# Whole numbers as weights for the last 128 inputs of batch 1's gate and up products

## The chip, the cores and the metric

The kernel runs on one core of a Trainium2 chip. The metric is the device time of one execution in microseconds. One core has TensorE (PE), VectorE (DVE), ScalarE (ACT), GpSimd (POOL) and SyncE (SP, which here only issues DMAs), each with its own queue of instructions in program order; they meet through semaphores.

## What is computed

Two layers on 2 batches of 512 tokens with 512 features. Each layer is an attention-like block and a feed-forward block, each between layer norms with a residual add. Layer 0's first block is a state space recurrence over the 512 tokens (1024 channels, 16 states); its second is a feed-forward network with 4-bit weights. Layer 1 has an attention over the heads of one token and a mixture-of-experts network. The part that the change is about, cut from the reference:

```python
w[k, n] = q[k, n] * s[g, n] - (z[g, n] + 1) * s[g, n]      # g = k // 128
gate = x2 @ Wg            # [tokens, 512] @ [512, 1376]
up = x2 @ Wu
inter = gate * sigmoid(gate) * up
out = (inter @ Wd).astype(float16)
```

The scale `s` depends on the group g of 128 inputs and on the output n. For one group, x @ W is therefore (x @ (q - z - 1)) times s, with whole numbers as weights.

## The kernel before

**Stages.** Up to about 480 us the recurrence runs: for 16 chunks (8 of each batch, 128 channels each) there are 8 pairs of scans on VectorE (`scan`), fed by ScalarE (`decay`, Exp) and GpSimd (`times_b`), and multiplied by C on VectorE or GpSimd (`times_c`). TensorE sums the states into the PSUM bank `Y_BANK` in four state groups a chunk, and the table `SIDE` says which other matmuls run in which chunk and group: ("out", 0, t) is tile t of batch 0's output projection (16 matmuls). `pair_of(item)` gives the pair at which an item stands, and ScalarE and GpSimd place their own steps by it (copy of the tile, sums, norms). `take_y` on VectorE reads the finished y of a chunk at the second pair of the next.

Then comes the quantized feed-forward, batch 0 (487 to 576 us) and batch 1 (576 to 670 us), then the last layer's network for both batches, with batch 1's attention within it.

**The feed-forward blocks.** The 1376 inner features are 11 blocks (`IC`) of 128. Weights are used as a sum of two float16 halves, and so are the inputs, so each product of 128 inputs takes three matmuls (`halves`: high by high, low by high, high by low) of 512 columns. A block i is: `g` (gate) of 4 x 3 matmuls into a bank of a ring of three, `u` (up) of 12, and the down-projection of block i-1 of 12, in this order on TensorE. A bank of the ring is free for the third next item once its reader has raised `taken`. ScalarE applies SiLU to `g` (`ffn_silu`, into `sg`), VectorE multiplies by `u` from PSUM (`ffn_times`, into `it`, L1440), ScalarE rounds it to float16 (`ffn_high`, `it_hi`, L2188), VectorE subtracts (`ffn_low`, `it_lo`, L1450), and the down-projection of the block waits for that.

**Weights.** Only in batch 0's blocks the weights are made: SP loads a stage (packed words `qw`, zero points and scales `cw`, 1.5 MB as broadcast) into one of four slots (`stage_again`, once the slot is free), VectorE unpacks nibbles (`unpack`, L1262), ScalarE converts (`whole`), VectorE subtracts the zero point (`scaled`, first half: now the slot's `cw[..., 0]` holds q - z - 1 as float16) and multiplies by the scale, ScalarE makes the high half, VectorE the low half. Batch 1 uses the same `gu_hi`, `gu_lo`, `d_hi`, `d_lo`. The scales of the first two blocks are split in two parts at the start of the kernel (`two_parts`, L1374 to L1377).

**Work between the blocks.** In batch 1's blocks VectorE and ScalarE also carry batch 0 on to the last layer: `between(0, i)` on VectorE is the feed-forward's norm and add (i 0 to 2), norms for the transposes (3, 4), attention scores (5), values (6), the attention's add (7) and statistics (8); ScalarE has the matching roots and the softmax's Exp, each with its activation table (`preload_act_table_set`). The order is written out by hand in both queues. TensorE transposes those tiles behind blocks 4 and 9 (`TURN_BEHIND`) and makes qkv in block 5. In batch 0's blocks ScalarE norms batch 1's tiles (`norm_ffn_last`, L1952), and TensorE transposes them one a block from block 7 (`TURN_FIRST`).

## Time and profile before

| | us |
|---|---|
| median of 3 runs | 805.58 |
| lowest and highest | 805.26, 806.01 |
| the profiled execution | 807.46 |
| its span on the core | 805.6 |

| engine | busy us | share of the span |
|---|---|---|
| TensorE, matmuls | 683.4 | 85% |
| VectorE | 688.1 | 85% |
| ScalarE | 469.8 | 58% |
| GpSimd | 480.6 | 60% |

The page gives one execution. Times in it are microseconds from the start of its span. A matmul of 512 columns is listed with a longer duration than the distance to the next one, because they are pipelined; the distance of the starts is what one costs. "[0.91 <-DVE it_lo L1450]" behind a row says that the engine was idle for 0.91 us before it and that the wait ended with that instruction of VectorE. Names are the tiles of the program, without buffer numbers; "x8" is the number of instructions merged into a row. PEclk is the granted clock of TensorE as a share of its full speed.

### The profile page before, as it was taken

How to read it: one execution, taken by the hardware profiler on the slowest of the kernel's cores; microseconds unless marked ns; L12 is line 12 of the kernel's file. 1: busy time of each engine (PE TensorE's matmuls, PEld its weight loads, DVE VectorE, ACT ScalarE, POOL GpSimd, SP SyncE). 2: the span in 40 equal slices, each digit the busy share in tenths (PEclk: the TensorE clock that was granted, in tenths of full speed). 3: DMA queues.
4: the chain of work that ended last, by engine and by line, in shares of the span. 5: the costliest groups of instructions: out<-in, count | busy, mean ns of one | idle time of the engine just before them, and what ended most of it. 6: DMA issues, size and time to landing. Idle time of an engine off the chain costs nothing. (4 is left out here: it accounts for less than half of the span.)

```text
span 805.6 us, 8451 instructions
## 1 busy us (share of the span) xinstructions
PE 683.4 (85%) x2794; PEld 325.1 (40%) x2794; DVE 688.1 (85%) x701; ACT 469.8 (58%) x805; POOL 480.6 (60%) x252
## 2 busy tenths in 40 slices
PE   7979899988687788564637889999999999999995
PEld 6623333323122222111112224444445556887885
DVE  6889999999999999999999998998274576485778
ACT  5478778895656774867664447756325347323333
POOL 2429999999999999999999960220002014331130
PEclk9999979999888997858867989999999999999998
DMA  8434232335503714731235309971040030000011
GB/s 262 92 101 142 75 129 71 119 130 180 186 4 120 246 37 158 229 131 36 96 131 179 102 12 259 256 221 55 1 157 1 1 105 0 1 1 1 0 53 52
DMA packets 42326, 83.19 MB, mean 103 GB/s; under 512 B 6809, under 2 KB 10308, under 8 KB 42028
## 3 DMA queue, kind: packets, MB, share of 16 engines
q1 hardware_dynamic: 42284, 82.66, 32.4%
q8 instruction: 22, 0.36, 0.2%
q14 instruction: 20, 0.16, 0.1%
HBM read 71.43 MB, written 11.21 MB: 103 GB/s over the span
## 5 line engine op out<-in xcount | busy, mean ns | idle before, releaser
L2388 POOL TENSOR_TENSOR dbu<-rep_du,bc 128x1024 f32<-128x1024 f32 x127 | 296.5, 2359 | 1.8 <-ACT rep_du L2054 0.9
L1880 ACT ACTIVATE psum<-rep_dt,aneg 128x512 f32<-128x512 f32 x256 | 166.2, 682 | 117.4 <-DVE hc L1230 96.1
L1219 DVE TENSOR_TENSOR_SCAN psum<-psum,dbu 128x1024 f32<-128x1024 f32 x89 | 203.4, 2285 | 3.4 <-ACT psum L1880 1.5
L970 PE MATMUL psum<-hc,stk 128*32 128x512 f32 x512 | 84.4, 736 | 62.1 <-POOL hc L2397 44.3
L1230 DVE TENSOR_TENSOR hc<-psum,bc 128x1024 f32<-128x1024 f32 x89 | 109.0, 1224 | 3.1
L2397 POOL TENSOR_TENSOR hc<-hc,bc 128x1024 f32<-128x1024 f32 x39 | 91.8, 2355 | 7.7 <-DVE hc L1219 7.7
L1219 DVE TENSOR_TENSOR_SCAN hc<-psum,dbu 128x1024 f32<-128x1024 f32 x39 | 89.0, 2281 | 1.0 <-ACT psum L1880 0.9
L709 PE MATMUL psum<-xf_hi,gu_hi 128*128 128x512 f16 x176 | 66.8, 379 | 0.4 <-ACT sg L2181 0.4
L709 PE MATMUL psum<-xf_hi,gu_lo 128*128 128x512 f16 x176 | 66.8, 379 | 0.0
L709 PE MATMUL psum<-xf_lo,gu_hi 128*128 128x512 f16 x176 | 66.8, 379 | 0.0
L709 PE MATMUL psum<-xT,w_g 128*128 128x512 f32 x120 | 58.7, 636 | 2.6 <-ACT rep_du L2025 2.6
L2465 POOL TENSOR_TENSOR h<-h 128x512 f32<-128x512 f32 x16 | 19.0, 1185 | 70.1 <-ACT h L2296 70.1
L970 PEld LDWEIGHTS psum<-hc,stk 128*32 128x32 f32 x512 | 13.0, 120 | 117.6 <-issue 61.3
L959 PE MATMUL psum<-u,diag 128*32 128x512 f32 x128 | 22.5, 781 | 29.5 <-DVE u L1246 19.9
L2188 ACT CAST it_hi<-it 128x512 f16<-128x512 f32 x22 | 13.6, 617 | 47.0 <-DVE it L1440 47.0
L709 PEld LDWEIGHTS psum<-xT,w_g 128*128 128x128 f32 x120 | 23.3, 204 | 39.5 <-issue 35.4
L1440 DVE TENSOR_TENSOR it<-sg,psum 128x512 f32<-128x512 f32 x22 | 15.0, 683 | 28.2 <-PE psum L709 11.3
L2449 POOL TENSOR_TENSOR w_up_lo<-w_up,w_up_hi 128x1024 fp32r<-128x1024 f32 x4 | 9.4, 2379 | 46.2 <-ACT w_up_hi L2173 46.2
L997 PE MATMUL psum<-d_hi,it_hi 128*128 128x512 f16 x88 | 33.4, 379 | 1.4 <-DVE it_lo L1450 1.4
L2436 POOL TENSOR_TENSOR x<-x,obuf 128x512 f32<-128x512 f32 x4 | 9.3, 2347 | 41.2 <-ACT obuf L1947 41.2
L709 PE MATMUL psum<-xT,w_x 128*128 128x512 f32 x64 | 32.3, 651 | 1.8 <-ACT xT L1764 1.4
L2443 POOL TENSOR_TENSOR w_gate_lo<-w_gate,w_gate_hi 128x32 fp32r<-128x32 f32 x1 | 0.3, 251 | 55.5 <-ACT w_gate_hi L2262 55.5
(305 smaller groups left out, 1453.0 us busy)
## 6 DMA issues: line engine op xcount, KB each, us to landing
rep_dt<-rep_scratch SPq DMA_DIRECT2D x60, 256.0 KB, 3.3
rep_du<-rep_scratch SPq DMA_DIRECT2D x60, 256.0 KB, 4.1
cw<-c_scratch SPq DMA_DIRECT2D x11, 768.0 KB, 12.0
qw<-qgu_in SPq DMA_DIRECT2D x11, 512.0 KB, 6.8
bc<-bc_scratch SPq DMA_DIRECT2D x16, 256.0 KB, 5.0
rep_scratch<-du_t SPq DMA_DIRECT2D x14, 256.0 KB, 2.0
rep_scratch<-dt_t SPq DMA_DIRECT2D x14, 256.0 KB, 2.3
qw<-qd_in SPq DMA_DIRECT2D x11, 256.0 KB, 8.1
```

What stands on the lines that cost most here:

```text
L709: last = pe.matmul(bank(item)[0:rows, cols], lhsT, rhs, start=(n == 0), stop=(n == len(parts) - 1))
L959: last = pe.matmul(y_rows(k), diag[:, k * P // KH:(k + 1) * P // KH], u[b][:, c, :], start=True, stop=False)
L970: last = pe.matmul(y_rows(k), stk[:], hc[:, (i + k // 2) % HCS, k % 2, :], start=False, stop=(s == GN - 1))
L997: last = pe.matmul(psum[:, t, :], v, w, start=(i == 0 and n == 0), stop=(i == IC - 1 and n == 2))
L1219: dve.tensor_tensor_scan(h, a, dbu[:, i % DBS].rearrange("p e t -> p (e t)"), 0.0, ALU.mult, ALU.add)\
L1230: dve.tensor_tensor(hc[:, i % HCS], psum[:, two, :], bc[:, GN + n, :].unsqueeze(1).broadcast_to([P, 2, L]), ALU.mult)\
L1440: dve.tensor_tensor(it[:, k % 2, :], sg[:, k % 2, :], bank(("u", b, i)), ALU.mult)\
L1880: last = act.activation(psum[:, 2 * (i % 2) + e, :], rep_dt[:, cc % 2, k, :], ACT.Exp, scale=aneg[:, k, c, n:n + 1])
L2188: act.copy(it_hi[:, k % 2, :], it[:, k % 2, :]).then_inc(ithi_done, 1)
L2388: pool.tensor_tensor(dbu[:, i % DBS], rep_du[:, cc % 2, k:k + 2, :], bc[:, n, :].unsqueeze(1).broadcast_to([P, 2, L]), ALU.mult).then_inc( ...
L2397: pool.tensor_tensor(hc[:, i % HCS], hc[:, i % HCS], bc[:, GN + n, :].unsqueeze(1).broadcast_to([P, 2, L]), ALU.mult)\
L2465: pool.tensor_tensor(h2[:, k % 2, :], h1[:, k % 2, :], h1[:, k % 2, :], ALU.mult)\
```

## The change

Five edits.

1. The scale splits at the start work on one tile (`s_two`, 12 rows of 256), loaded by two more DMAs, instead of on two tiles. Four VectorE instructions stand where eight stood, and 10 stores where 8 stood.
2. Output tile 3 of batch 0 is computed in state group 2 of chunk 9 instead of group 3. What follows it on ScalarE and GpSimd keeps its place (`OUT_LAST`).
3. `norm_ffn_last` of tiles 0 and 1 moves from block 6 to block 7.
4. For blocks 1 to 10 the whole numbers of the last 128 inputs are copied out of the slot before it is loaded anew (`keep_ints`, 64 KB each), and their scales are loaded transposed, one per output feature (`group16`).
5. In batch 1, blocks 1 to 10, `g` and `u` have 9 matmuls each over the first 384 inputs. The last 128 go through `group_part`: two matmuls with the whole numbers (exact in float16) into `Y_BANK`; ScalarE multiplies the result by the scale of the feature (`group_scaled`) into `sg` or `it`; VectorE adds the bank (`gate_sum`, `up_sum`); SiLU now works on `sg`, and `times_sum` multiplies `sg` by `it`. The places of `gate_sum` and `group_scaled` in the hand-written orders differ by block, two steps of `between` move, and the sum over wq stands ahead of block 0.

```diff
-        (9, 1): [("out", 0, 2)], (9, 3): [("out", 0, 3)],
+        (9, 1): [("out", 0, 2)], (9, 2): [("out", 0, 3)],
...
+OUT_LAST = pair_of(("out", 0, NT - 1)) + 2
...
+        s_two = at("s_two", 205, [AHEAD * P], F16)
+        sa = at("sa", 88.25, [AHEAD * P], F16)
+        sb = at("sb", 88.75, [AHEAD * P], F16)
...
+        ints = {i: at(f"ints{i}", 35 + (i - 1) / 2 if i < 9 else {9: 21.25, 10: 24}[i], [2 * P], F16)
+                for i in range(1, IC)}
+        group16 = at("group16", 206.625, [2, IC], F16)
+        group32 = at("group32", 206.75, [2, IC])
...
                     sp_.wait_ge(split_done, 2)
+                    half = KH // AHEAD
                     sp_.dma_start(c_dram[0:AHEAD, 1, 0:gu].rearrange("i (r n) -> r i n", n=P),
-                                  sa_gu[0:2 * KH, :].rearrange("r (i n) -> r i n", n=P)).then_inc(z_stored, 16)
-                    sp_.dma_start(c_dram[0:AHEAD, 1, gu:], sa_d[0:AHEAD, :]).then_inc(z_stored, 16)
+                                  sa[0:2 * KH, :].rearrange("r (i n) -> r i n", n=P)).then_inc(z_stored, 16)
                     sp_.dma_start(cs_dram[:, 0:gu].rearrange("i (r n) -> r i n", n=P),
-                                  sb_gu[0:2 * KH, :].rearrange("r (i n) -> r i n", n=P)).then_inc(z_stored, 16)
-                    sp_.dma_start(cs_dram[:, gu:], sb_d[0:AHEAD, :]).then_inc(z_stored, 16)
+                                  sb[0:2 * KH, :].rearrange("r (i n) -> r i n", n=P)).then_inc(z_stored, 16)
+                    for i in range(AHEAD):
+                        rows = slice(2 * KH + half * i, 2 * KH + half * (i + 1))
+                        sp_.dma_start(c_dram[i, 1, gu:].rearrange("(r n) -> r n", n=AHEAD * P), sa[rows, :])\
+                            .then_inc(z_stored, 16)
+                        sp_.dma_start(cs_dram[i, gu:].rearrange("(r n) -> r n", n=AHEAD * P), sb[rows, :])\
+                            .then_inc(z_stored, 16)
...
+            def keep_ints(i):
+
+                sp_.wait_ge(q16_used, i + 1)
+                sp_.dma_start(ints[i][:], cw[i % SLOTS][:, 0, 2 * (KH - 1) * P:2 * KH * P]).then_inc(ints_kept, 16)
+
             def stage_again(i):
 
+                if i > SLOTS:
+                    sp_.wait_ge(ints_kept, 16 * (i - SLOTS))
                 sp_.wait_ge(wlo_gu, i - SLOTS + 1)
                 sp_.wait_ge(wlo_d, i - SLOTS + 1)
                 stage(i)
 
             wait_work(sp_, ("out", 1, NT - 1))
             stage(3)
+            keep_ints(1)
             for i in range(SLOTS, IC):
                 stage_again(i)
+                if i > SLOTS:
+                    keep_ints(i - SLOTS + 1)
+            sp_.wait_ge(ints_kept, 16 * (IC - SLOTS))
+            keep_ints(IC - 3)
...
+            keep_ints(IC - 2)
+            keep_ints(IC - 1)
+            for j in range(2):
+                sp_.dma_start(group16[:, j, :], sgu_in[2 * (KH - 1) + j:2 * KH - 1 + j, :]
+                              .rearrange("r (i n) -> n (r i)", n=P),
+                              allow_slow_non_contiguous=True).then_inc(ld_group, 16)
...
+                def group_part(i, j):
+
+                    if i > 1 or j:
+                        pe.wait_ge(group_done, 2 * (i - 1) + j)
+                    else:
+                        pe.wait_ge(ints_kept, 16 * (IC - 1))
+                    w = ints[i][:, j * P:(j + 1) * P]
+                    pe.matmul(psum[:, Y_BANK, :], w, xf_hi[1][:, KH - 1, :], start=True, stop=False)
+                    pe.matmul(psum[:, Y_BANK, :], w, xf_lo[1][:, KH - 1, :], start=False, stop=True)\
+                        .then_inc(group_ready, 1)
...
-                        for kk in range(KH):
+                        for kk in range(KH - 1 if grouped else KH):
                             w = slice((2 * kk + j) * P, (2 * kk + j + 1) * P)
                             parts += halves(gu_hi[:, i, w], gu_lo[:, i, w], xf_hi[b][:, kk, :],
                                             xf_lo[b][:, kk, :])
+                        if grouped:
+                            group_part(i, j)
                         product(item, parts).then_inc(work_ready, 1)
...
+            def two_parts(rows):
+
+                t, d, s = sp_t[0:rows, :], sp_d[0:rows, :], s_two[0:rows, :]
+                link(dve.tensor_scalar(t, s, SPLIT, None, ALU.mult))
+                link(dve.tensor_tensor(d, t, s, ALU.subtract))
+                dve.tensor_tensor(sa[0:rows, :], t, d, ALU.subtract).then_inc(split_done, 1)
+                dve.wait_ge(split_done, 1)
+                dve.tensor_tensor(sb[0:rows, :], s, sa[0:rows, :], ALU.subtract).then_inc(split_done, 1)
...
+            def gate_sum(i):
+                k = IC + i
+                item = ("g", 1, i)
+                wait_work(dve, item)
+                dve.wait_ge(group_done, 2 * i - 1)
+                dve.tensor_tensor(sg[:, k % 2, :], bank(item), sg[:, k % 2, :], ALU.add).then_inc(taken_sem(item), 1)
+
+            def up_sum(i):
+                k = IC + i
+                item = ("u", 1, i)
+                wait_work(dve, item)
+                dve.wait_ge(group_done, 2 * i)
+                dve.tensor_tensor(it[:, k % 2, :], bank(item), it[:, k % 2, :], ALU.add).then_inc(taken_sem(item), 1)
+
+            def times_sum(i):
+                k = IC + i
+                dve.wait_ge(silu_done, i)
+                wait_taken(dve, ("u", 1, i))
+                dve.tensor_tensor(it[:, k % 2, :], sg[:, k % 2, :], it[:, k % 2, :], ALU.mult).then_inc(it_done, 1)
...
+                if b == 0:
+                    gate_sum(6)
...
+                if b == 0:
+                    gate_sum(7)
...
                 if i == 1:
-                    ffn_inv16(b)
-                    ffn_add16(b, 0)
-                    ffn_add16(b, 1)
+                    if b == 0:
+                        ffn_add16(b, 1)
+                        ffn_add16(b, 2)
+                    else:
+                        ffn_inv16(b)
+                        ffn_add16(b, 0)
+                        ffn_add16(b, 1)
                 if i == 2:
-                    ffn_add16(b, 2)
+                    if b:
+                        ffn_add16(b, 2)
                     ffn_add16(b, 3)
...
+            dve.wait_ge(ld_att, 16 * 7)
+            dve.tensor_reduce(wqkv[:, :, 0:DH], wqraw[:], AX.X, ALU.add).then_inc(wq_done, 1)
+            dve.tensor_reduce(bqkv[:, 0:DH], bqraw[:], AX.X, ALU.add).then_inc(wq_done, 1)
+            dve.wait_ge(ld_group, 32)
+            dve.tensor_copy(group32[:], group16[:]).then_inc(group_set, 1)
             for i in range(IC):
+                if i and i not in (6, 7, 8):
+                    gate_sum(i)
                 if i == IC - 1:
                     low_moe(0, [2, 3])
-                ffn_times(1, i)
+                if i:
+                    up_sum(i)
+                    if i == 1:
+                        ffn_inv16(0)
+                        ffn_add16(0, 0)
+                    times_sum(i)
+                else:
+                    ffn_times(1, i)
                 if i == 9:
                     norm_tile("moe", 0, 2, xnc)
                     norm_tile("moe", 0, 3, xnc)
                 ffn_low(1, i)
-                if i == 0:
-                    dve.wait_ge(ld_att, 16 * 7)
-                    dve.tensor_reduce(wqkv[:, :, 0:DH], wqraw[:], AX.X, ALU.add).then_inc(wq_done, 1)
-                    dve.tensor_reduce(bqkv[:, 0:DH], bqraw[:], AX.X, ALU.add).then_inc(wq_done, 1)
                 if i < 8:
                     between(0, i)
                 if i == 7:
+                    gate_sum(8)
                     between(0, 8)
...
+            def group_scaled(i, j):
+
+                k = IC + i
+                if i == 1:
+                    act.wait_ge(group_set, 1)
+                act.wait_ge(group_ready, 2 * (i - 1) + j + 1)
+                if j:
+                    act.wait_ge(itlo_done, k - 1)
+                act.activation((it if j else sg)[:, k % 2, :], psum[:, Y_BANK, :], ACT.Identity,
+                               scale=group32[:, j, i:i + 1]).then_inc(group_done, 1)
+
+            def ffn_silu_sum(i):
+
+                k = IC + i
+                wait_taken(act, ("g", 1, i))
+                act.activation(sg[:, k % 2, :], sg[:, k % 2, :], ACT.Silu).then_inc(silu_done, 1)
...
+                if b == 1 and i >= 1:
+                    if i - 1 not in (0, 2, 5, 6, 8):
+                        group_scaled(i, 0)
+                        group_scaled(i, 1)
+                    ffn_silu_sum(i)
+                else:
+                    ffn_silu(k)
                 if k == 0:
...
-                if k in (TURN_FIRST - 1, TURN_FIRST + 1):
-                    first = k - TURN_FIRST + 1
+                if k in (TURN_FIRST, TURN_FIRST + 1):
+                    first = 2 * (k - TURN_FIRST)
...
+                    if i in (2, 5, 6, 8):
+                        act.preload_act_table_set(LOG_EXP)
+                    if i == 8:
+                        root(("moe", 0), NT)
+                    if i in (0, 2, 5, 6, 8):
+                        group_scaled(i + 1, 0)
+                        group_scaled(i + 1, 1)
                     if i == 0:
                         root16(0)
-                    if i in (2, 5, 6, 8):
-                        act.preload_act_table_set(LOG_EXP)
                     if i == 2:
                         root(("att", 0), NT)
                     if i == 5:
                         att_exp(0)
                     if i == 6:
                         root(("atto", 0), NT)
-                    if i == 8:
-                        root(("moe", 0), NT)
```

## Rows read from the trace of the kernel before

**Rows 1.** busy time by stages: engine, busy us (instructions), granted clock, DMA share, GB/s
```profile
50.00:540.00 490.00, 386.53 (x1392) 132.35 (x1391) 474.77 (x332) 334.34 (x561) 420.46 (x205) 0.87 0.43 136
577.00:669.00 92.00, 91.60 (x457) 45.09 (x455) 52.68 (x100) 39.99 (x60) 9.99 (x7) 1.00 0.16 58
```

**Rows 2.** chain of work that ended last: start us, us, what
```profile
669.56 5.51 PE psum L709 x24
```

**Rows 3.** timeline of TensorE, start of batch 1's block 0: start us, us, engine, line
```profile
576.21 0.38 PE L709 MATMUL psum<-xf_hi,gu_hi 128*128 128x512 f16 x1
576.43 0.38 PE L709 MATMUL psum<-xf_hi,gu_lo 128*128 128x512 f16 x1
```

**Rows 4.** timeline of VectorE, start-up
```profile
44.29 0.28 DVE L1374 TENSOR_SCALAR sp_t<-zs 8x256 f32<-8x256 f16 x1
...
48.62 0.68 DVE L1253 TENSOR_TENSOR ssmn<-ssm,psum 64x512 f32<-64x512 f32 x1
```

**Rows 5.** timelines of ScalarE and VectorE, up to the first scan
```profile
47.27 0.59 ACT L1838 ACTIVATE psum<-rr 64x512 f32<-64x512 f32 x1
...
57.34 2.30 DVE L1219 TENSOR_TENSOR_SCAN psum<-psum,dbu 128x1024 f32<-128x1024 f32 x1 [0.54 <-ACT psum L1880]
```

**Rows 6.** timelines of TensorE, VectorE and GpSimd around output tile 3
```profile
316.24 1.94 PE L970 MATMUL psum<-hc,stk 128*32 128x512 f32 x8 [3.83 <-POOL hc L2397]
318.11 8.80 PE L709 MATMUL psum<-wout,g 128*128 128x512 f32 x16
...
327.98 0.69 DVE L1246 TENSOR_TENSOR u<-u,psum 128x512 f32<-128x512 f32 x1 [1.50 <-PE psum L970]
...
330.94 2.35 POOL L2397 TENSOR_TENSOR hc<-hc,bc 128x1024 f32<-128x1024 f32 x1 [1.88 <-DVE hc L1219]
```

**Rows 7.** busy time by stretches, columns as rows 1
```profile
301.00:304.00 3.00, 3.00 (x16) 0.43 (x8) 3.00 (x2) 1.96 (x4) 3.00 (x2) 0.50 0.76 261
...
315.00:321.00 6.00, 4.76 (x12) 1.58 (x13) 5.96 (x4) 2.60 (x4) 6.00 (x4) 0.50 0.00 0
```

**Rows 8.** timelines of TensorE and ScalarE, batch 0's block 7
```profile
545.98 0.38 PE L997 MATMUL psum<-d_hi,it_hi 128*128 128x512 f16 x1 [0.91 <-DVE it_lo L1450]
...
547.80 0.59 ACT L2181 ACTIVATE sg<-psum 128x512 f32<-128x512 f32 x1
```

**Rows 9.** stage 1 on SP's queue, landing of its last load, unpacking in batch 0
```profile
446.36 0.57 SPq L504 DMA_DIRECT2D qw<-qgu_in  x1
...
cw<-c_scratch SPq DMA_DIRECT2D x1, 768.0 KB, 6.5
...
518.07 1.44 DVE L1262 TENSOR_SCALAR qw<-qw,shift 128x1536 int32<-128x1536 int32 x1
...
551.19 1.01 DVE L1262 TENSOR_SCALAR qw<-qw,shift 128x1536 int32<-128x1536 int32 x1
```

**Rows 10.** costliest groups of the page, an activation scaled per partition
```profile
L1880 ACT ACTIVATE psum<-rep_dt,aneg 128x512 f32<-128x512 f32 x256 | 166.2, 682 | 117.4 <-DVE hc L1230 96.1
```

**Rows 11.** timeline of VectorE, batch 1's blocks 7 and 8
```profile
646.30 2.50 DVE L1512 TENSOR_TENSOR x<-x,on 128x512 f32<-128x512 f32 x4
648.84 2.47 DVE L1159 BATCH_NORM_STATS2 bst<-x 128x6 f32<-128x512 f32 x4
...
651.76 0.69 DVE L1440 TENSOR_TENSOR it<-sg,psum 128x512 f32<-128x512 f32 x1
```

**Rows 12.** timeline of ScalarE, the same place
```profile
652.48 0.62 ACT L2188 CAST it_hi<-it 128x512 f16<-128x512 f32 x1 [7.29 <-DVE it L1440]
653.12 1.28 ACT L2267 ACT_TABLE_LOAD   x1
654.41 0.30 ACT L1753 ACTIVATE std<-mv,epst 128x4 f32<-128x4 f32 x1
```

**Rows 13.** timeline of VectorE, norms with and without GpSimd beside them
```profile
610.07 2.90 DVE L1186 TENSOR_SCALAR xnc<-x,mv,rstd 128x512 f32<-128x512 f32 x2
...
614.92 1.00 DVE L1186 TENSOR_SCALAR xnc<-x,mv,rstd 128x512 f32<-128x512 f32 x2
```

More of the change, by code:

```diff
@@ L532, in _ @@
             load(shifts[:], shifts_in, ld_z)
+            load(s_two[0:2 * KH, :], sgu_in[:, 0:AHEAD * P], ld_z)
+            load(s_two[2 * KH:2 * KH + KH, :], sd_in[0:AHEAD, :].rearrange("a (r n) -> (a r) n", n=AHEAD * P), ld_z)
             for k in range(KH):
@@ L635, in _ @@
             wait_taken(sp_, ("out", 0, NT - 1))
-            sp_.wait_ge(z_stored, 128)
+            sp_.wait_ge(z_stored, 160)
             stage(0)
@@ L2088, in _ @@
                         take_turned("ssm", 1, t, xT)
-                    if i == pair_of(("out", 0, t)) + 4:
+                    if i == (pair_of(("out", 0, t)) if t < NT - 1 else OUT_LAST) + 4:
                         take_out(t)
@@ L2123, in _ @@
                     inv_rms(1)
-                last = pair_of(("out", 0, NT - 1))
+                last = OUT_LAST
                 if i == last + 4:
@@ L2141, in _ @@
                     squares(("ffn", 0), t, x[:, t, :])
-                if i in (pair_of(("out", 0, NT - 1)) + 8, pair_of(("out", 0, NT - 1)) + 9):
-                    first = 2 * (i - pair_of(("out", 0, NT - 1)) - 8)
+                if i in (OUT_LAST + 8, OUT_LAST + 9):
+                    first = 2 * (i - OUT_LAST - 8)
                     for t in range(first, first + 2):
@@ L2428, in _ @@
                         dt_times_u(k)
-                t = i - pair_of(("out", 0, NT - 1)) - 9
+                t = i - OUT_LAST - 9
                 if 0 <= t < NT:
```

35 lines of the change are left out of this document (17 added, 18 removed).

## Prediction

> **What bounds the kernel now.** I read the table by stages first, then the chain of work that ended last, then the timelines of single engines where the diff touches them. The recurrence over time steps (to 480 us) is bound by VectorE, busy 474.8 of the 490 us shown, with GpSimd close behind at 420.5 [rows 1]. From 577 to 669 us, batch 1's quantized feed-forward, TensorE is busy 91.6 of 92 us at a granted clock of 1.00 while VectorE is busy 52.7 and ScalarE 40.0 [rows 1]. The chain runs through TensorE there and leaves it at 669.56, where that stage ends [rows 2]. Everything behind hangs on that end, so I carry a shift of it 1:1 to the end of the kernel. A 512-column matmul of this stage starts 0.216 us after the one before it, though it is listed with 0.38 us [rows 3]: 0.216 is the price of one. What could be gained is TensorE's time, and the slack of the other two is an average that the new waits have to be tested against one by one.
>
> **Part 1, splits in one tile.** Eight small VectorE instructions become four. The old ones run from 44.29 to 47.9, the first four of them in 1.4 us; the new four, on 12 rows instead of 8, cost about the same as those, so VectorE is free 2.2 us sooner. The instruction that counts, `ssmn` at 48.62 [rows 4], also needs ScalarE's Exp, which starts at 47.27 and takes 0.59 [rows 5], so it can start at 47.88: -0.74 us. The first scan at 57.34 waits for ScalarE, not for a load [rows 5], and moves along. SP issues 10 small stores instead of 8 ahead of the `bc` loads; two more at about 0.3 us use up nearly all the slack of the first `bc` load (its data is wanted at 54.84 then), which I count as nothing because the scan is released by ScalarE 0.5 us later. The two added loads early on are 30 us ahead of their use. Bounds 0 and -0.74; I take **-0.7**.
>
> **Part 2, output tile 3 a state group ahead.** Now its 16 matmuls run at 318.11 for 8.80 us, in the group just before the y of that chunk is read, and VectorE stands idle 1.50 us at 327.98, GpSimd 1.88 us at 330.94 [rows 6]. They took that long because TensorE had stood idle for 3.83 us until 316.24 and the granted clock was 0.50 up to 321 [rows 6, 7]; at the full level the same 2.9 us of work would take 1.45 less, 7.35 in all. One group earlier they start at 312.4, right behind other work, and end about 319.7, the sums of that group at 320.8; the next to wait on those sums is VectorE's product at 321.8. So the 1.50 us go and nothing new is late. GpSimd is the one that then sets the pace and shifts too. Bounds 0 (another stall takes its place) and -1.5; I take **-1.4**.
>
> **Part 3, norms a block later (batch 0).** The two norms make `it_hi(6)` late, and TensorE starts block 7's down-projection at 545.98 with 0.91 us listed as idle, 1.07 counted in starts [rows 8]. Without them `it_hi(6)` is 0.9 us earlier. But in block 7 they stand behind the SiLU that now starts at 547.80 [rows 8]; moved up to about 547.0 that gives the first normed tile at 548.2, and TensorE, through at 547.5, turns that tile next: a new wait of 0.7. Net **-0.2** (bounds -1.1 and +0.2).
>
> **Part 4, keeping the whole numbers (SP's queue, batch 0).** From the sixth stage of weights on, SP may load stage i+1 only when a 64 KB copy issued behind stage i has landed. Four stages used to be in flight; now they go one at a time. A stage with nothing ahead of it is issued at 446.36 and its last load, issued 1.26 us later, takes 6.5 us: 7.8 us in all [rows 9]; with some 0.35 us for the copy a round takes 8.15. VectorE unpacks the stages at 518.07 (sixth) to 551.19 (tenth), 8.28 us apart [rows 9]. That nearly fits, the first of them without slack. Bounds 0 (round of 7.8) and +5 (round of 9.0, five times 0.9 less the slack); I take **+0.6**. The transposing load of scales (two of 1408 two-byte elements, issued near 558 and wanted near 578 to 581) is hidden unless it takes over 20 us; the trace has no such load.
>
> **Part 5, batch 1's blocks.** Removed: one matmul of twelve in 20 products, 20 x 0.216 = **-4.32 us**; a block is 34 x 0.216 = 7.34 us instead of 7.78. Added per block: two ScalarE scalings (0.68 each, as the nearest row with a scale per partition [rows 10]) and two more VectorE instructions of 0.69 (as the product [rows 11]). By busy time both fit. The order does not. There is one PSUM bank for the whole-number products, so TensorE's second product of block i (`group_part(i,1)`, 11 matmuls = 2.38 us into the block) waits until ScalarE has scaled the first, and that scaling stands in ScalarE's queue behind `it_hi(i-1)`, which waits for VectorE's product of block i-1, which waits for whatever VectorE does between blocks. Until now that lateness cost nothing, since only the down-projection needed it, half a block later. Behind TensorE's wait stand all its matmuls.
>
> I laid out the three queues from 576.21, instruction by instruction in the new order, each at the later of its engine's last end and its inputs, with durations from the rows; the same for the kernel before ends at 668.99 against 669.56 in the trace [rows 2, 3]. The worst place is block 9. In the kernel before, VectorE goes through the attention add (2.50), the statistics (2.47) and the product of block 8 at 651.76; ScalarE follows with `it_hi` at 652.48, a table load of 1.28, Ln and Exp, to 654.9 [rows 11, 12]. A scaling put there, as the diff does (behind `root`), ends at 655.6 at the earliest. In the new order gate_sum(8) and up_sum(8) are in that stretch as well, and block 7 comes half a microsecond late: product at 653.4, `it_hi` 654.1, table, Ln and Exp to 656.5, scaling done 657.2. TensorE is ready for it at 653.2: a wait of 4.05 us. The others, the same way: block 2 0.54, block 3 0.25, block 4 1.17 (late after the norms, which GpSimd's use of SBUF stretches, 2.90 us for two against 1.00 without it [rows 13]), blocks 5 and 10 0.13 each, block 7 1.61 (scaling behind the softmax's table load), block 8 1.60 (behind the SiLU that waits for the attention's norm), and 1.27 before the last down-projection. Sum 10.75, less the 0.14 that the layout has before: -4.32 + 10.61 = **+6.3 us**. Low bound: only block 9's, from 655.6 with 16.6 us of TensorE work behind it, 672.2 against 669.56: +2.7. High bound: each wait 0.3 longer, +9.
>
> The clock: the idle 3.83 us before 316.24 went with a granted clock of 0.50 over 315 to 321 [rows 6, 7], the level of 1.2 GHz, and 301 to 304 was such a stretch as well [rows 7]. So the 4 us wait of block 9 may be followed by 3 us at half speed, which costs 1.5, or by 6, which costs 3. Bounds 0 and 3; since my gap is itself uncertain, and part of the loss would fall into the wait before the last down-projection, I take **+1.0**. The Trainium skill ("TensorE: Matmul & The Clock Gate", "Why this matters for your kernels") asks for no idle gaps beyond about 3 us between bursts; by that rule the loss is certain, the whole 1.5 would be due, and the time 0.5 us longer; the row at 316.24 agrees. The Trainium skill ("SBUF — State Buffer", "Who interferes with whom") also says that a two-input VectorE instruction with both inputs in SBUF blocks against GpSimd's reads. The old product reads PSUM, the new `times_sum` reads SBUF twice; the rows of the norms show the blocking for another instruction. In my layout no `times_sum` meets a GpSimd instruction, so the sum stays; if two did, some 2 us would be added.
>
> **Sum.** -0.7 - 1.4 - 0.2 + 0.6 + 6.3 + 1.0 = +5.6 us. The profiled execution took 807.46 us (span 805.6 and 1.9 around it) and would take 813.1. The median of the runs is 1.9 us below the profiled one; from 805.58 it gives **811.2 us**.
>
> **Rivals.** (a) The matmuls come off whole: the scalings are always in time. 805.58 - 0.7 - 1.4 - 0.2 - 4.3 = 799.0. For it speaks the low busy share of ScalarE; against it the rows from 651.76 to 654.9, which hold even with no added work. (b) Only block 9's wait stays, the others are taken up by slack: 805.58 - 2.1 + 0.4 + 2.7 = 806.6. It needs VectorE a microsecond faster than its rows between blocks 1 and 7. (c) The stages of weights, now one at a time, run at 9 us a round and batch 0's blocks wait for them: +4.5 more, 815.7. For it speaks that six loads used to overlap; against it the 7.8 us of a lone stage. It decides from a round of 8.3 us on. (d) Parts 1 and 2 bring nothing because GpSimd holds the recurrence: 813.3, inside my forecast.
>
> **How the numbers follow.** Forecast with (d) 0.67, (a) 0.06, (b) 0.15, (c) 0.12. The range reaches from (b)'s lower half, 804.5, to just past (c)'s centre, 816. Same means within 1.6 us of 805.58, about what a measurement here can tell: (b) lies mostly in it. Faster 0.08, same 0.13, slower 0.79.
>
> **What would show it.** Right: in batch 1 TensorE waits for ScalarE's scaling, one gap near 4 us in block 9, seven or eight smaller ones, busy share of the stage near 90%, a half-clock stretch behind block 9; at chunk 10's start no VectorE idle time; the stage's end some 3 to 5 us later than now. Wrong: gaps under 1 us in blocks 7 to 9 (then (a) or (b)), or VectorE waiting for loads in batch 0 (then (c)).

## The result and the profile after

| kernel | median us | runs | ratio to before (95%) |
|---|---|---|---|
| before | 805.8 | 805.26 to 809.37 | |
| changed | 816.69 | 811.79 to 819.63 | 1.0118 (1.0091 to 1.0145) |
| changed, measured again (below) | 814.92 | 811.22 to 817.96 | 1.011 (1.0087 to 1.0132) |

The change makes the kernel 1.1% slower, some 9 us. (The ratios here and below are taken over the single runs against runs of the kernel before made beside them; they are not the quotients of the medians.) The first median lies 0.7 us above the forecast range, the second inside it. The profiled execution is the shortest of its four: 811.79 us, span 809.9, so it shows only +4.3 us of span against the one of before. The rest of the 9 us has to be found elsewhere.

TensorE in batch 1's feed-forward. First the stage (columns as rows 1), then every wait of TensorE there (timeline: start us, us, engine, line, operation, idle time before it and what ended it), then the stretches behind the longest wait:

```profile
577.00:675.00 98.00, 87.41 (x426) 42.07 (x424) 62.91 (x118) 51.81 (x77) 10.38 (x7) 0.98 0.15 54
...
589.52 0.38 PE L1046 MATMUL psum<-xf_hi,ints 128*128 128x512 f16 x1 [0.54 <-ACT sg L2283]
597.36 0.38 PE L1046 MATMUL psum<-xf_hi,ints 128*128 128x512 f16 x1 [0.35 <-ACT sg L2283]
605.95 0.38 PE L1046 MATMUL psum<-xf_hi,ints 128*128 128x512 f16 x1 [1.09 <-ACT sg L2283]
635.06 0.38 PE L1046 MATMUL psum<-xf_hi,ints 128*128 128x512 f16 x1 [1.60 <-ACT sg L2283]
644.00 0.38 PE L1046 MATMUL psum<-xf_hi,ints 128*128 128x512 f16 x1 [1.44 <-ACT sg L2283]
655.68 0.58 PE L1046 MATMUL psum<-xf_hi,ints 128*128 128x512 f16 x1 [4.19 <-ACT sg L2283]
672.71 0.39 PE L1035 MATMUL psum<-d_hi,it_hi 128*128 128x512 f16 x1 [1.39 <-DVE it_lo L1522]
...
656.00:658.00 2.00, 2.00 (x6) 0.73 (x5) 0.60 (x1) 1.25 (x2) 0.00 (x0) 0.50 0.35 134
658.00:660.00 2.00, 2.00 (x9) 0.83 (x8) 0.41 (x1) 1.35 (x2) 0.00 (x0) 0.89 0.00 0
```

Where rows 1 has TensorE busy for all but 0.4 of 92 us, it is now idle 10.6 of 98. Six waits end with `group_scaled(i, 0)` (L2283): TensorE wants the one bank for the second product of the block. The chain of waits through block 9 (start us, us, what) is the one that the forecast laid out from rows 11 and 12:

```profile
650.98 0.70 DVE it L1507
...
651.77 0.70 DVE it L1513
...
652.50 0.62 ACT it_hi L2300
653.13 1.28 ACT L2383
654.43 0.30 ACT std L1845
...
654.87 0.68 ACT sg L2283
655.55 0.14 issue
655.68 0.58 PE psum L1046
656.27 0.43 PE psum L1047
656.70 2.86 PE psum L747 x9
...
672.71 2.76 PE psum L1035 x12
```

VectorE's last add and product of block 8, then `it_hi(8)`, the table load, Ln, Exp (short, between 654.76 and 654.87) and only then the scaling. Behind the gap two whole-number matmuls take 1.01 us and nine matmuls 2.86; a product later the same take 0.43 and 1.94. That is the half clock: 1.5 us.

The stage, by the chain: it began at 576.38 and ended at 669.56 before (93.18 us), and runs from 574.02 to 675.47 now (101.45): +8.3 us. Batch 1 starts 2.4 us sooner. What stands behind the stage took 1.6 us less, because in the one execution of before the granted clock was 0.60 from 704 to 708 us and here it stayed up; that is chance, since what stands behind the stage takes 134.4 to 134.5 us in twelve of the fourteen traces of this study, and 136.0 in that of before and in one other. So -2.4 + 8.3 - 1.6 = +4.3. The runs differ by 9 because the changed kernel's profiled execution was a lucky one (experiment on the spread, below).

### The profile page after: what moved, and what is told of

The parts are those of the page before. It is cut to its first block and busy times, and to the rows that moved or that the text cites. A ratio compares the mean times of both kernels' runs of the same rounds, so it can differ in the third digit from the quotient of the medians.

```text
span 809.9 us, 8502 instructions
## 1 busy us (share of the span) xinstructions
PE 680.2 (84%) x2774; PEld 322.9 (40%) x2774; DVE 698.0 (86%) x718; ACT 483.9 (60%) x825; POOL 481.4 (59%) x252
## 5 line engine op out<-in xcount | busy, mean ns | idle before, releaser
L1008 PE MATMUL psum<-hc,stk 128*32 128x512 f32 x512 | 82.0, 718 | 55.5 <-POOL hc L2518 41.5
L747 PE MATMUL psum<-xf_hi,gu_hi 128*128 128x512 f16 x156 | 59.6, 382 | 0.0
L747 PE MATMUL psum<-xf_hi,gu_lo 128*128 128x512 f16 x156 | 59.5, 381 | 0.0
L747 PE MATMUL psum<-xf_lo,gu_hi 128*128 128x512 f16 x156 | 59.4, 381 | 0.0
L1035 PE MATMUL psum<-d_lo,it_hi 128*128 128x512 f16 x88 | 33.3, 379 | 0.0
L1035 PE MATMUL psum<-d_hi,it_lo 128*128 128x512 f16 x88 | 33.3, 379 | 0.0
```

Source lines behind the costliest of these rows:

```text
L747: last = pe.matmul(bank(item)[0:rows, cols], lhsT, rhs, start=(n == 0), stop=(n == len(parts) - 1))
L1008: last = pe.matmul(y_rows(k), stk[:], hc[:, (i + k // 2) % HCS, k % 2, :], start=False, stop=(s == GN - 1))
L1035: last = pe.matmul(psum[:, t, :], v, w, start=(i == 0 and n == 0), stop=(i == IC - 1 and n == 2))
```

## The experiments

Theory: TensorE waits for the shared bank, because both products of a block go through it and ScalarE's scaling stands behind late work; 60 matmuls fewer and 40 whole-number ones more are worth 4.3 us at most. Rivals: the added work as such, the serial loads of weights, and the clock.

Each profiled execution, by the chain and the timelines of its own trace; "near 289" is VectorE's wait for TensorE's sums there, "batch 0" the time from batch 0's first product to batch 1's start, "stage" batch 1's feed-forward:

| kernel | near 289 | batch 0 | batch 1 starts | stage | ends | span |
|---|---|---|---|---|---|---|
| before | none | 89.57 | 576.38 | 93.18 | 669.56 | 805.6 |
| changed | none | 91.41 | 574.02 | 101.45 | 675.47 | 809.9 |
| changed again | 3.17 | 91.09 | 579.80 | 101.81 | 681.61 | 816.1 |
| block 9's scaling ahead | 2.23 | 89.34 | 576.98 | 97.51 | 674.49 | 810.5 |
| all ahead | 0.16 | 90.75 | 576.81 | 98.35 | 675.16 | 809.7 |
| gate only | none | 90.38 | 573.50 | 95.11 | 668.61 | 803.1 |
| three blocks | none | 89.44 | 573.06 | 91.24 | 664.30 | 798.7 |
| three blocks again | 0.28 | 90.41 | 572.49 | 91.24 | 663.73 | 798.2 |
| three blocks, tile 2 moved | 1.34 | 90.83 | 578.00 | 91.24 | 669.24 | 803.7 |
| parts 1 to 3 | none | 89.46 | 574.09 | 92.84 | 666.93 | 801.4 |
| keep only | 1.87 | 89.46 | 577.58 | 94.87 | 672.45 | 806.9 |
| 60 matmuls out | 1.75 | 90.96 | 580.81 | 91.37 | 672.18 | 806.6 |
| part 1 | 2.22 | 89.46 | 577.13 | 92.83 | 669.96 | 804.5 |
| part 2 | none | 89.46 | 574.67 | 93.18 | 667.85 | 802.3 |

### One instruction moved in block 9

```diff
+                if b == 1 and i == 8:
+                    group_scaled(i + 1, 0)
                 ffn_high(k)
...
                     if i in (0, 2, 5, 6, 8):
-                        group_scaled(i + 1, 0)
+                        if i != 8:
+                            group_scaled(i + 1, 0)
                         group_scaled(i + 1, 1)
```

> The changed kernel with one instruction moved: ScalarE scales the first whole-number product of block 9 ahead of it_hi of block 8 and of the table load, Ln and Exp of the MoE norm, no longer behind them. My theory: the 4.19 us wait of TensorE in block 9 and the 3.4 us at the half clock behind it go. By the queues laid out by hand the stage ends 2.8 us earlier (VectorE and the second scaling are late next, the wait before the last down-projection grows), and the clock gives back up to 1.7: 812.2 us against the changed kernel's median of 816.7, or 807.3 against its profiled 811.8. Rival A: the wait only moves to the next product, 816. Rival B: half-clock stretches started by this gap are also what the runs differ by; then the runs lie close together, near 807.

Median 811.32 us (ratio 1.007, 1.0049 to 1.0091). Its timelines of ScalarE and TensorE, and the same two stretches:

```profile
652.56 0.69 ACT L2283 ACTIVATE sg<-psum,group 128x512 f32<-128x512 f32 x1 [0.82 <-PE psum L1047]
655.47 0.62 ACT L2300 CAST it_hi<-it 128x512 f16<-128x512 f32 x1 [2.22 <-DVE it L1513]
...
665.20 0.39 PE L1046 MATMUL psum<-xf_hi,ints 128*128 128x512 f16 x1 [0.59 <-DVE sg L1500]
671.72 0.39 PE L1035 MATMUL psum<-d_hi,it_hi 128*128 128x512 f16 x1 [1.39 <-DVE it_lo L1522]
...
656.00:658.00 2.00, 1.91 (x9) 0.70 (x8) 0.72 (x2) 1.94 (x5) 0.00 (x0) 1.00 1.00 382
658.00:660.00 2.00, 2.00 (x13) 1.20 (x12) 2.00 (x4) 1.97 (x3) 0.00 (x0) 1.00 0.85 327
```

ScalarE was idle for 2.22 us behind the moved scaling, so it had only stood in the wrong place of the queue. The 4.19 us wait is gone, 1.0 of it came back at 663.35 (0.41, a transpose) and 665.20 as waits for VectorE, and the granted clock stays at 1.00. The stage is 3.9 us shorter, of 4.5 expected; against the changed kernel measured again the median is 3.6 lower (the ratios say 3.2). One misplaced instruction carries some 40% of the loss. Rival A falls. Rival B had the time near 807 and falls with it; the runs do lie close together (810.5 to 812.6), but they are only five.

### All scalings ahead

```diff
+                if b == 1 and 1 <= i < IC - 1:
+                    group_scaled(i + 1, 0)
                 ffn_high(k)
```

The later `group_scaled(i, 0)` of blocks 2 to 10 go; block 1's stays.

> The changed kernel with the scaling of the first whole-number product ahead of it_hi of the block before in blocks 2 to 10, so that ScalarE no longer delays TensorE's second product anywhere. My theory: the waits at blocks 2, 3, 4, 7, 8 and 9 go (9.2 us in the profiled execution), but the down-projections then wait for VectorE's chain and for the later it_hi, so the layout by hand gives back only 1.8 us of the 10.6, plus up to 1.7 from the clock: 813 us against the median of 816.7, busy share of TensorE in the stage near 92 to 94%. Rival: the single bank and its place in ScalarE's queue are all there is to it; then 9 us come back and the kernel takes 807 or, in the profiled execution, 802 to 803.

810.79 us (1.0066, 1.0044 to 1.0088), the stage 98.35. TensorE's longer waits now (the 1.39 before the last down-projection is unchanged, and one of 0.68 before the transposes behind block 4 is new):

```profile
636.20 0.38 PE L1046 MATMUL psum<-xf_hi,ints 128*128 128x512 f16 x1 [1.12 <-ACT sg L2283]
646.55 0.46 PE L1046 MATMUL psum<-xf_hi,ints 128*128 128x512 f16 x1 [2.85 <-ACT sg L2283]
664.67 1.26 PE L741 MATMUL psum<-ident,xnc 128*128 128x128 f32 x8 [0.73 <-DVE xm_lo L1369]
```

The rival (nine us come back) is refuted. The waits of blocks 2, 3 and 9 are gone and that of block 4 is down to 0.26, but block 8's has grown from 1.44 to 2.85, because a scaling put ahead of `it_hi` makes `it_hi` and all behind it later. Its gap is followed by a stretch at the half clock as well (648 to 650). Neither of the two orders tried in ScalarE's queue serves both products in all blocks.

### Whole numbers for the gate products alone

```diff
-                        for kk in range(KH - 1 if grouped else KH):
+                        for kk in range(KH - 1 if grouped and j == 0 else KH):
...
-                        if grouped:
+                        if grouped and j == 0:
                             group_part(i, j)
```

`up_sum` and the second scaling are left out, and `times_sum` multiplies `sg` by the bank.

> The changed kernel with whole-number weights for the gate products alone; the up products of batch 1 keep their twelve matmuls and are multiplied straight from PSUM as before. So one product a block goes through the single whole-number bank, and TensorE needs it back a whole block later instead of half a block; VectorE has 0.7 us less added per block. My theory (the wait for the bank within a block is the cause): the waits for ScalarE in blocks 2, 3, 4, 7, 8 and 9 are gone, VectorE's chain leaves some 3.3 us of waits in blocks 7 to 10, ten matmuls saved are 2.2; by the layout the stage takes 94.3 us, 7 less than in the changed kernel and 1 more than before. With parts 1 to 3 (-1.1 measured) and part 4 (+1.0 measured) the time is 806.5 (ratio 1.001). Rival: the added ScalarE and VectorE work as such costs, in proportion to its amount; half of it is left, so half of the 8.1 us by which the changed stage is longer: stage 97.4, time 809.5.

806.08 us, ratio 0.9997 (0.9977 to 1.0018), 806.5 expected and 809.5 by the rival. All waits of TensorE in its stage:

```profile
652.41 0.39 PE L1035 MATMUL psum<-d_hi,it_hi 128*128 128x512 f16 x1 [1.28 <-DVE it_lo L1524]
656.72 0.39 PE L1046 MATMUL psum<-xf_hi,ints 128*128 128x512 f16 x1 [0.67 <-DVE it L1514]
660.67 0.39 PE L747 MATMUL psum<-xf_hi,gu_hi 128*128 128x512 f16 x1 [0.53 <-DVE sg L1500]
```

No wait for ScalarE's scaling is left with the same bank, the same line and half the products. By the amount of work half of the 9.2 us of such waits would be left. With the two experiments before it, where the same work in another order changed the waits, this puts the cause on the second use of the bank within a block. What stays is VectorE's chain. (The stage took 95.11 where 94.3 was expected; the clock averages 0.93 over 616 to 640 in this trace, worth about 1.7, with no long wait ahead of it.)

### Sixty matmuls left out, nothing added

```diff
-                        for kk in range(KH):
+                        for kk in range(KH - 1 if b == 1 and i >= 1 else KH):
```

In the kernel before; gate and up of batch 1's blocks 1 to 10 lack the last 128 inputs, 3 matmuls in each of 20 products.

> The kernel before with one matmul of twelve left out in each of the 20 products of batch 1's blocks 1 to 10 (the last 128 inputs enter without the third matmul's and with none of their products: all three of theirs are left out, so 9 stay) is not what is run here in full: the loop over inputs ends one early, so each of the 20 products has 9 matmuls instead of 12 and the last 128 inputs are missing from gate and up. Nothing is added. It shows what TensorE's time is worth when neither ScalarE nor VectorE has more to do. Theory of the forecast's rival (a): TensorE is the bound whatever its length, 60 matmuls x 0.216 = 13.0 us come off, 792.5. My theory: ScalarE's SiLU and VectorE's chain are late next; by the layout with 11 matmuls instead of 12 only 1.9 of 4.3 us come off, so with 9 at most half of 13.0 does, 799 or more, with new waits for ScalarE's sg in most blocks.

803.41 us, ratio 0.9965 (0.9949 to 0.9982): 2.9 us come off, not 13.0, and TensorE waits where it never did:

```profile
596.76 0.39 PE L709 MATMUL psum<-xf_hi,gu_hi 128*128 128x512 f16 x1 [2.35 <-ACT sg L2181]
612.44 0.61 PE L709 MATMUL psum<-xf_hi,gu_hi 128*128 128x512 f16 x1 [2.35 <-ACT sg L2181]
647.38 0.39 PE L709 MATMUL psum<-xf_hi,gu_hi 128*128 128x512 f16 x1 [2.05 <-ACT sg L2181]
657.99 0.39 PE L997 MATMUL psum<-d_hi,it_hi 128*128 128x512 f16 x1 [1.75 <-DVE it_lo L1450]
```

TensorE was 99.6% busy [rows 1] and yet a free removal of a seventh of its work in that stage gives a fifth of its price by the medians, and less by the traces (stage 91.37 for 93.18). ScalarE's SiLU behind the norms' table loads is next in line at once. So the forecast's rival (a), -4.3 us whole, was out of reach even with no added work.

### Three blocks

```diff
-                    grouped = b == 1 and i >= 1
+                    grouped = b == 1 and 1 <= i <= 3
...
+                if b == 1 and 1 <= i < 3:
+                    group_scaled(i + 1, 0)
                 ffn_high(k)
```

The other `gate_sum`, `up_sum`, `group_scaled` and `keep_ints` go with it.

> The changed kernel with whole-number weights in blocks 1 to 3 of batch 1 alone, where VectorE and ScalarE have little other work, three kept copies instead of ten, and in blocks 2 and 3 the scaling of the first product ahead of it_hi of the block before. My theory: no wait of TensorE for ScalarE's scaling is left, six matmuls (1.3 us) come off whole, the stage takes 92.0 us against 93.35 before. With parts 1 to 3 (-1.1 measured; -2.3 by the traces) 803.2 us, ratio 0.997, between 0.995 and 0.999. Rival: shorter blocks only bring the old waits for the SiLU forward (before shows one of 0.40 in block 2), and the stage stays at 93.0 or more, 804.5.

Three of its twelve runs took 1021, 1161 and 2318 us; the median of the other nine is 802.48 us (803.58 with the three), ratio 0.9964 (0.9947 to 0.9981). The stage is 91.24 us with no wait of TensorE in it, 1.6 less than with parts 1 to 3 alone (six matmuls are 1.3). Because of the three runs it was measured again:

> The kernel with whole-number weights in blocks 1 to 3 alone, once more and unchanged, on whatever chip comes: three of its twelve runs took 1021 to 2318 us (granted clock 0.55 to 1.00), which no other kernel of this study showed. Theory 1: a disturbance of that chip in that hour; then all runs lie between 800 and 808 us, the ratio between 0.994 and 0.998, batch 1's stage at 91.2 us. Theory 2: the kernel itself starts something; then runs beyond 1000 us come again.

804.58 us (800.08 to 808.83), ratio 0.9975 (0.9954 to 0.9996), stage 91.24 again, and no such run; what the three were stays open. It is faster than before by about 0.3%. Parts 1 to 3, which it contains, have a ratio of 0.9983 alone (next experiment), and the times don't tell the two apart; that the three blocks themselves gain rests on the stage, 91.24 in three traces against 92.84.

### Parts 1 to 3, and 1 and 2 alone

The kernel before with the first three edits of the change:

```diff
+            two_parts(2 * KH + KH)
...
+        (9, 1): [("out", 0, 2)], (9, 2): [("out", 0, 3)],
...
+                if k in (TURN_FIRST, TURN_FIRST + 1):
```

> The kernel before with the first three parts alone: scale splits in one tile, output tile 3 a state group earlier, the two norms of batch 0 a block later. No whole-number weights, all matmuls as before. My theory: these parts act as in the trace of the changed kernel, where batch 1's feed-forward started 2.2 us earlier in spite of a batch 0 that took 2.0 us longer. The recurrence alone gives 2.1 to 2.7 us (0.04 to 0.6 at the start, 1.5 at the output tile), plus perhaps 1.5 to 2 us if the half-clock stretch that the kernel before shows around 478 to 486 us is gone here too. So 805.6 - 2.3 = 803.3 us, ratio 0.997; with the clock stretch gone 801.6. Rival: GpSimd or a transfer takes the place of the stalls and nothing comes of it, 805.6. Second rival, for the open 5 us between the profiled run of the changed kernel and its median: the earlier output tile is what makes the runs uneven; then this kernel's runs spread over several us as well, with a median above 805.

804.44 us, ratio 0.9983 (0.9963 to 1.0003).

The first of the three lines alone:

> The kernel before with part 1 alone (scale splits in one tile: four VectorE instructions instead of eight, ten small stores on SP's queue instead of eight). Forecast: -0.7 us, the first scan 0.7 us earlier (56.6), 804.8 where the kernel before takes 805.5. Theory from the traces of the changed kernel and of parts 1 to 3: ssmn waits 1.6 to 1.8 us for ScalarE where it waited for nothing, and what was saved is lost again to ScalarE's dt_t (wait of dt_t 1.2 instead of 0.48) or to the bc load, so the distance from ssmn's start to the first scan grows from 8.72 us to 9.4; the time is unchanged, ratio 0.999 to 1.001.

805.65 us, ratio 0.998 (0.996 to 1.0001); the runs of before beside it have a median of 807.09.

The second alone:

> The kernel before with part 2 alone (output tile 3 a state group earlier, with what follows on its turn). Forecast: VectorE's 1.50 us of idle time ahead of the read of y near 328 us and GpSimd's 1.88 us go, no new wait behind them, -1.4 us: ratio 0.998. With part 1 worth nothing, all of the 1.1 us (ratio 0.9983) that parts 1 to 3 gave together comes from here. Rival: it comes from the norms a block later (part 3), whose wait of 0.91 us before the down-projection at 545.98 is 0.20 in the traces; then part 2 alone shows 1.000 and batch 1 starts where it did.

806.23 us, ratio 0.9982 (0.9962 to 1.0002), beside the same runs of before.

Each interval touches 1, so the times decide nothing between them. The traces show what moved, in one execution each. Start-up of part 1 alone, VectorE:

```profile
47.95 0.68 DVE L1259 TENSOR_TENSOR ssmn<-ssm,psum 64x512 f32<-64x512 f32 x1 [1.58 <-ACT psum L1844]
...
55.60 1.22 DVE L1414 TENSOR_TENSOR dbu<-psum,bc 128x1024 f32<-128x1024 f32 x1 [0.86 <-DMA bc<-bc_scratch]
56.95 2.30 DVE L1225 TENSOR_TENSOR_SCAN psum<-psum,dbu 128x1024 f32<-128x1024 f32 x1
```

`ssmn` is 0.67 earlier than in rows 4, the first scan 0.39 earlier than in rows 5. The scan no longer waits for ScalarE, but the product ahead of it waits 0.86 for the `bc` load, which the two added stores hold back (0.77 in the changed kernel, whose first scan stands at 57.30). In the trace of parts 1 to 3 it is ScalarE's `dt_t` instead (1.21, before 0.48), and the first scan stands at 57.70, later than before. Of the 0.7 us 0.4 arrives in one of three traces and nothing in the others. With part 2 alone VectorE reads y at 326.31 and waits for nothing, where it waited 1.50, and GpSimd waits 0.41 where it waited 1.88 [rows 6]; batch 1 starts 1.7 us earlier. But a start differs by more than that between two executions of the changed kernel (574.02 and 579.80).

### Keeping the whole numbers, alone

The kernel before, with

```diff
+                if i > SLOTS:
+                    sp_.wait_ge(ints_kept, 16 * (i - SLOTS))
...
+                if i > SLOTS:
+                    keep_ints(i - SLOTS + 1)
```

and the rest of that part.

> The kernel before with part 4 alone: the ten 64 KB copies of whole numbers behind their stages on SP's queue, with their waits, and the two transposing loads of scales; nobody uses what they bring, and batch 1 computes as before. My theory as forecast: +0.6 us, 806.2 (a round of 8.15 us). By the trace of the changed kernel, where batch 0 took 91.4 us instead of 89.4 and the stages were issued 8.1 to 8.6 us apart: +2.0, 807.6. Rival: the serial stages are also what makes the changed kernel's median 5 us longer than its profiled execution; then this kernel shows 810 to 813 us and a spread of several us.

806.5 us, ratio 1.002 (1.0 to 1.0039). Batch 0 took 89.46 us, as before (89.57), so by this trace the copies cost nothing; the interval allows up to 3 us. Over the whole table batch 0 takes 89.3 to 91.4 us in the six traces with all ten copies (mean 90.4) and 89.5 to 91.0 in the five with none (mean 89.8). The rival (810 to 813, and a spread of its own) falls. What serial stages can do stands in the next trace.

### The changed kernel again, and the spread

No edit.

> The changed kernel itself once more, beside the other variants on one chip, because its four runs so far lay between 811.8 and 819.6 us while the kernel with one instruction moved in block 9 lay between 810.5 and 812.6. Theory 1: the spread is chance (half-clock stretches in the recurrence, which the kernel before and every variant show as well); then the median is the variant's 811.3 plus the 3.9 us by which the stages differ in the traces (101.45 against 97.51), about 815, with runs from 811 to 819. Theory 2: the long gap of block 9 itself starts half-clock stretches of varying length behind it; then the stage of the profiled execution differs from 101.45 by over 1 us, and the spread is again larger than for the other kernels of this call. Theory 3: the first runs were on a worse chip; then 811 to 812, as profiled then.

814.92 us, 815 expected by theory 1; the stage differs from the first trace by 0.36 us, so theory 2 falls, and theory 3 as well. TensorE's wait ahead of output tile 0, that tile, VectorE's wait behind it, and the stretch, in this trace:

```profile
277.52 1.94 PE L1008 MATMUL psum<-hc,stk 128*32 128x512 f32 x8 [2.90 <-POOL hc L2518]
279.38 9.10 PE L747 MATMUL psum<-wout,g 128*128 128x512 f32 x16
...
289.64 2.29 DVE L1271 TENSOR_TENSOR_SCAN hc<-psum,dbu 128x1024 f32<-128x1024 f32 x1 [3.17 <-PE psum L1008]
...
274.00:282.00 8.00, 5.11 (x19) 1.41 (x12) 7.93 (x5) 5.04 (x10) 8.00 (x5) 0.66 0.78 262
```

The same 16 matmuls took 7.13 us in the first trace and in that of before, with no wait. Here the granted clock was 0.66 over 274 to 282 us. It is the picture of rows 6 and 7, three tiles earlier. A wait of 1.3 us or more stands there in six of the fourteen profiled executions, of kernels with and without part 5 alike, and those six start batch 1 at 577.0 to 580.8 us, the other eight at 572.5 to 576.8. In the six TensorE had stood idle for 2.39 to 3.29 us ahead of the tile and its 16 matmuls took 7.77 to 9.10 us; in the eight it had stood idle for 0.64 to 2.51 us and they took 7.13. The wait goes with the longer executions; that it makes all of their difference isn't shown (other waits of the recurrence vary too). Such differences are why one profiled execution on each side showed only half of the loss.

In batch 0 of the same trace, SP's queue (issue of the first load of a stage) and VectorE's waits:

```profile
491.40 0.56 SPq L516 DMA_DIRECT2D qw<-qgu_in  x1
...
500.32 0.54 SPq L516 DMA_DIRECT2D qw<-qgu_in  x1
...
512.88 0.55 SPq L516 DMA_DIRECT2D qw<-qgu_in  x1
...
499.92 1.02 DVE L1314 TENSOR_SCALAR qw<-qw,shift 128x1536 int32<-128x1536 int32 x1 [1.81 <-DMA cw<-c_scratch]
...
507.83 1.02 DVE L1314 TENSOR_SCALAR qw<-qw,shift 128x1536 int32<-128x1536 int32 x1 [1.89 <-DMA cw<-c_scratch]
```

Rounds of 8.9 and 12.6 us instead of 8.15, and VectorE waits for loads: rival (c)'s mechanism. The second of these rounds takes 9.9 to 12.7 us in all nine traces with copies and 7.2 to 10.0 in the five without. Batch 0 took 1.5 us longer than before here and 1.8 longer in the first trace of the changed kernel. But the trace with 60 matmuls out, whose stages are not serial, has such a wait of 2.10 and a batch 0 just as long. How much of this the copies cause stays open; the 5 us of rival (c) are in none of the fourteen traces.

### One tile that missed

> The kernel with whole-number weights in blocks 1 to 3 alone, and output tile 2 a state group earlier as well. In the longer executions of every kernel (the changed kernel again, keep only, part 1 alone) the 16 matmuls of that tile near 279 us ran partly at the half clock, took 8.8 to 9.1 us instead of 7.13, and VectorE waited 2.2 to 3.2 us for the sums near 289; in the shorter ones it waited for nothing or 0.3. Theory: this wait is a good part of what runs differ by, and a group earlier it can't arise, as with tile 3 in part 2. Then the median falls by about 1 us against the same kernel without the edit (ratios 0.9964 and 0.9975), ratio 0.9955, and the runs lie closer together than 800 to 809. Rival: another place of the recurrence takes its turn (the group at (9, 0) already holds a product), ratio 0.997 or more and the same spread.

```diff
-        (9, 1): [("out", 0, 2)], (9, 2): [("out", 0, 3)],
+        (9, 0): [("out", 0, 2)], (9, 2): [("out", 0, 3)],
```

803.66 us, ratio 0.9953 (0.9928 to 0.9978), not to be told from three blocks without it. The expectation names the wrong tile: what runs at 279 us is output tile 0, in group 1 of chunk 8 (it is the first of the four times 16 matmuls on `wout` in the trace), and this edit left it alone. The wait near 289 is there (1.34). Whether moving tile 0 would narrow the spread was not tried.

## Why the prediction was right, and where not

- **Direction and cause: right.** 811.2 us forecast, 816.7 and 814.9 measured, slower, by the mechanism named: the shared bank behind ScalarE's queue. The size was 3 to 4 us short.
- **The seven big waits: right one by one.** Laid out 0.54, 0.25, 1.17, 1.61, 1.60, 4.05, 1.27; measured 0.54, 0.35, 1.09, 1.60, 1.44, 4.19, 1.39, together 10.6 for 10.5. The small ones of 0.13 don't show. The layout also gave 2.8 us for moving block 9's scaling, 4.5 with the clock; 3.9 was measured.
- **Part 5's size: 0.5 us short.** The forecast has itself that 0.91 listed is 1.07 from start to start, and then compared layout times with listed ones. Seven waits by 0.16 are 1.1 us, and 0.4 of it is made up by a wait of before that goes and was laid out too short. Thus 93.18 - 0.56 (the wait at 592.32 in the trace of before, 0.40 listed, that goes) - 4.32 + 10.6 + 1.1 + 1.5 (clock) = 101.5; measured 101.45. Without the clock that is +6.8 for +6.3.
- **The clock: 1.5 for 1.0.** The whole loss fell due, as the traces now show behind gaps of 4.19 us (0.50 over 656 to 658) and 2.85 us (0.50 over 648 to 650). Discounting it was wrong. The rule of the Trainium skill ("TensorE: Matmul & The Clock Gate", "Why this matters for your kernels"), no idle gaps beyond about 3 us, had the first; the second is a little shorter than it names. But of the two gaps of 2.35 us with 60 matmuls out only the second has a lower clock behind it (0.57 over 612 to 616), and in gate only and keep only the clock fell within 616 to 640 with no such gap.
- **Part 1: wrong.** The step "two more at about 0.3 us use up nearly all the slack of the first `bc` load ... which I count as nothing" failed: in two of three traces the load became the wait, 0.77 and 0.86.
- **Parts 2 and 3: the waits go, the gain is not shown.** They go as laid out (1.50 to 0; 0.91 to 0.20 with a new 0.41). But the 1.50 of rows 6 is a wait that only some executions have: with part 1 alone the read of y near 328 waits for nothing and GpSimd waits 1.69, and GpSimd waits 1.69 there in the changed kernel measured again as well. Part 3's two shifts cancel: batch 0 takes 89.46 us with it (parts 1 to 3) and without it (part 2 alone).
- **Part 4: open.** +0.6 forecast; +1.0 by the medians, +1.6 by the ratio with an interval from 0 to 3, +0.6 by the mean of batch 0's lengths. The round of 8.15 us that it was worked out from was too short for the first stages (8.9 and 12.6 above).
- **SBUF contention: as forecast,** the ten `times_sum` take 691 to 693 ns each.
- **Rival (c)'s number, not its mechanism.** The medians lie nearer to its 815.7 than to 811.2, and the sign named for it, VectorE waiting for loads in batch 0, did appear (1.81 and 1.89). But batch 0 is at most 1.8 us longer than before in any trace with copies, and batch 1's stage 8.3.
- **The sum.** Batch 1's stage came to +8.3 for +7.3 forecast (6.3 and the clock's 1.0). Parts 1 to 4 were forecast at -1.7; measured apart, parts 1 to 3 gave -1.4 and part 4 +1.6 by the ratios (-1.1 and +1.0 by the medians), so about nothing together, each uncertain by 1.6. That makes some 8.4 of the 9 us, and the rest is noise.
- **The profiled execution: luck.** One such execution was taken to stand 1.9 us above the median on either side. The changed kernel's stood 3 to 5 below its own, so that its 811.79 lies near the 813.1 forecast for it says nothing.

## What to carry to other kernels

An engine that is busy 99.6% of a stage isn't worth its busy time: before an edit shortens it, lay out the in-order queues of its neighbours, with durations from the trace. A buffer used twice within a block puts the other engine's latency into the block; used once, it has the whole block to hide it. Where a transformation pays only while its helpers are idle, apply it to those blocks alone (three of ten here: -0.3% instead of +1.1%, of which the first three parts alone give 0.2%), and read several executions before a difference under 1% is put down to an edit.

## What was not expected of the hardware

- The same 16 float32 matmuls took 7.13 us in eight executions and 7.8 to 9.1 in six others of the same or a like kernel, with the granted clock over 274 to 282 us at 1.00 in the eight and down to 0.66 in the six. At one place this decides whether VectorE waits 0 or 3.17 us.
- Runs of one kernel spread over 1% (before: 803.8 to 814.3 in 108 timed runs) with the mean granted clock of the run from 0.93 down to 0.90.
